# Part of a gather by GpSimd moved to single-row transfers issued by SyncE and ScalarE, in a three-layer graph kernel

## The reference

```python
def _sage_conv(x, src, dst, Wl, bl, Wr):
    agg = jax.ops.segment_max(x[src], dst, num_segments=x.shape[0])
    agg = jnp.where(jnp.isfinite(agg), agg, 0.0)
    return agg @ Wl + bl + x @ Wr
h = jnp.maximum(_layernorm(x, axis=-1), 0.0)
h = leaky_relu(_sage_conv(h, src, dst, Wl1, bl1, Wr1), 0.01)   # 128 -> 256 features
h = leaky_relu(_sage_conv(h, src, dst, Wl2, bl2, Wr2), 0.01)   # 256 -> 256
h = leaky_relu(_sage_conv(h, src, dst, Wl3, bl3, Wr3), 0.01)   # 256 -> 128
out = x + h
```

## Time and profile before

| | |
|---|---|
| median of the three runs | 6152.48 us |
| the profiled execution's own time | 6149.21 us |
| its span, first to last instruction | 6147.2 us |
| POOL busy | 4599.8 us, 75% |
| VectorE busy | 2902.2 us, 47% |
| ScalarE busy | 227.5 us, 4% |
| TensorE busy | 685.4 us, 11% |
| indirect gathers from the feature table | 4692, mean 946 ns |
| DMA moved | 1088.81 MB, 177 GB/s over the span |

### The profile page before, as it was taken

The page is one execution under the profiler, slowest core; times in us unless marked ns, Lnnn a source line. Parts: engine busy times, 40 slices in busy tenths (PEclk is TensorE's granted clock), DMA queues, the critical chain, the costliest instruction groups (busy, mean ns, idle before and its releaser), DMA issues.

```text
span 6147.2 us, 24451 instructions
## 1 busy us (share of the span) xinstructions
PE 685.4 (11%) x2214; PEld 394.3 (6%) x2214; DVE 2902.2 (47%) x3636; ACT 227.5 (4%) x663; POOL 4599.8 (75%) x4874
## 2 busy tenths in 40 slices
PE   0111111111100770000000000056000000000003
PEld 0000000000000430000000000044000000000002
DVE  4333333333333555555555555565555555555556
ACT  1000000000000110000000000011000000000001
POOL 6777777777777777777777777767777777777776
PEclk7555555555555655555555555565555555555556
DMA  4333333333333576666666666667666666666665
GB/s 139 106 109 106 107 107 106 107 107 105 109 104 106 183 234 209 210 210 211 208 211 211 209 210 211 210 213 244 211 211 208 209 211 209 211 208 211 210 208 177
DMA packets 434294, 1088.81 MB, mean 177 GB/s; under 512 B 100294, under 2 KB 152779, under 8 KB 434267
## 3 DMA queue, kind: packets, MB, share of 16 engines
q0 software_dynamic: 206976, 530.17, 30.6%
q1 hardware_dynamic: 204506, 539.02, 23.5%
q10 hardware_dynamic: 22784, 19.34, 1.0%
HBM read 555.06 MB, written 533.07 MB: 177 GB/s over the span
## 4 chain that ended last, share of the span: by engine, by line
POOL 49%; issue 16%; DMA 1%; POOLq 1%; DVE 0%; PE 0%
POOL ring L396 47%; POOL ring L423 2%; POOLq L393 0%; DMA ring<-features,stage 0%; POOLq L390 0%; DMA patch<-running_max_log,patch_row 0%; DMA ring<-running_max_log,end_row 0%; DMA running_max_log<-patch 0%; POOL patch L413 0%; PE banks L987 0%; POOLq L403 0%; POOLq L392 0%; DVE z_sum L841 0%; DMA features<-h_out 0%; DVE ring L731 0%
## 5 line engine op out<-in xcount | busy, mean ns | idle before, releaser
L396 POOL DMA_INDIRECT ring<-features,stage x4692 | 4436.4, 946 | 1456.0 <-issue 1411.4
L731 DVE TENSOR_TENSOR ring<-banks,ring 128x1024 f32<-128x1024 f32 (+1 forms) x1173 | 1226.6, 1046 | 3047.3 <-DMA ring<-features,stage 3030.1
L703 DVE TENSOR_TENSOR banks<-ring,banks 128x1024 f32<-128x1024 f32 (+1 forms) x1173 | 1231.9, 1050 | 37.5
L956 PE MATMUL banks<-ident,ring 128*128 128x128 f32 x20 | 5.0, 427 | 3762.1 <-DVEq L743 3762.1
L930 PE MATMUL banks<-dst_low,own 128*128 128x394 bf16 x200 | 96.0, 480 | 1466.6 <-DVE own L679 1466.6
L956 PEld LDWEIGHTS banks<-ident,ring 128*128 128x128 f32 x20 | 3.9, 222 | 3763.5 <-DVEq L743 3537.2
L914 PE MATMUL banks<-wr,h_turned 128*128 128x256 f32 (+1 forms) x490 | 201.9, 554 | 96.0 <-ACT h_turned L1048 96.0
L1092 ACT ACTIVATE agg<-zeros 128x512 f32<-128x512 f32 x75 | 47.3, 630 | 3944.1 <-PE banks L987 3944.0
L423 POOL DMA_INDIRECT ring<-running_max_log,end_row x147 | 141.5, 962 | 65.4 <-issue 43.9
L684 DVE COPY stage<-edges 128x8 int32 (+1 forms) x588 | 137.2, 233 | 84.8 <-DVE banks L703 25.8
L916 PE MATMUL banks<-b,ones 1*128 1x256 f32 (+1 forms) x294 | 138.8, 568 | 0.0
(11 more groups left out here) (112 smaller groups left out, 566.5 us busy)
## 6 DMA issues: line engine op xcount, KB each, us to landing
running_max_log<-ring SPq DMA_DIRECT2D x782, 512.0 KB, 3.3
running_max_log<-ring SPq DMA_DIRECT2D x391, 256.0 KB, 2.2
ring<-features,stage POOLq DMA_INDIRECT x4692, 2.8
h_in<-features ACTq DMA_DIRECT2D x98, 128.0 KB, 2.7
features<-h_out SPq DMA_DIRECT2D x48, 256.0 KB, 2.3
h_in<-features ACTq DMA_DIRECT2D x49, 64.0 KB, 1.8
out<-h_out SPq DMA_DIRECT2D x24, 128.0 KB, 2.5
ring<-running_max_log,end_row POOLq DMA_INDIRECT x147, 2.9
```

The lines of the kernel that those rows point to most:

```text
L396: pool.indirect_dma_start(ring[:, c * w:(c + 1) * w], None, tables[l], bass.IndirectOffsetOnAxis(ap=stage[:, b, u:u + 1].bitcast(U32), axi ...
L703: dve.tensor_tensor(sum_ps[:, 0:CHAINS * w].rearrange("p (h f) -> p h f", h=CHAINS), group(g - 1).rearrange("p (h f) -> p h f", h=CHAINS), ...
L731: dve.tensor_tensor(group(g), sum_ps[:, 0:CHAINS * w], group(g), ALU.max).then_inc(turn, 1)
```

## The change

In each of the 27 full steps of a layer 160 rows are no longer gathered by POOL: the 128 rows of column 55 and the last 32 rows of column 54. SyncE fetches the first 72 of them and ScalarE the other 88, each by a DMA of its own of one row, whose place in the table is read from SBUF into a register. POOL gathers 54 full columns and the first 96 rows of column 54. The last step of a layer stays as it was.

The places are prepared once: two DMAs with one word per descriptor bring the row numbers of the 27 steps into `row_list` (27 x 160), and VectorE multiplies them by the row size in bytes into `row_at` for each of the two widths. VectorE waits for the rows of both engines ahead of the maximum at g = 13. SyncE issues its rows in nine parts of 8, one behind each of the step's first nine log stores. ScalarE issues its 88 rows in eight parts of 11, ahead of keep_pair of the same number; so keep_pair is now done once per step in all layers.

```diff
+SYNC_ROWS, SYNC_AT_ONCE = 72, 8
+ACT_AT_ONCE = 11
+ROWS = 160
...
+    ROWS_OF = [(0, SYNC_ROWS), (SYNC_ROWS, ROWS - SYNC_ROWS)]
+    FETCHED = [DMA * count for _, count in ROWS_OF]
+    def by_pool(b, last):
+        return width(b, last) - (b == BLOCKS - 1 and not last)
...
+        def row_places(k, engine, i, at, count, w):
+            first = ROWS_OF[k][0] + at
+            _, places = nc.values_load_multi_w_load_instructions(
+                bass.at_runtime_partition(row_at[w][0:1, first:first + count], i), engines=[engine],
+                min_val=0, max_val=(nodes - 1) * w * 4,
+                skip_runtime_bounds_check_because="src numbers rows of the feature table")
+            return places
+        def table_row(l, w, place):
+            return tables[l].rearrange("n f -> (n f)").bitcast(U8)[bass.ds(place, 4 * w)].rearrange("(a b) -> a b", a=1)
+        def row_slot(k, r, w):
+            before, p = divmod(ROWS_OF[k][0] + r, P)
+            c = RING_COLS - 1 - before
+            p += before * (2 * P - ROWS)
+            return ring[p:p + 1, c * w:(c + 1) * w].bitcast(U8)
...
POOL, gather:
-                        for u in range(width(b, last)):
+                        for u in range(by_pool(b, last)):
                             c = b * BLOCK_COLS + u
+                            rows = 2 * P - ROWS if c == RING_COLS - 2 and not last else P
                             pool.indirect_dma_start(
-                                ring[:, c * w:(c + 1) * w], None, tables[l],
+                                ring[0:rows, c * w:(c + 1) * w], None, tables[l],
...
VectorE, preparation and scan_step:
+            dve.wait_ge(list_loaded, 2 * DMA)
+            for w in widths:
+                dve.tensor_scalar(row_at[w][:, :], row_list[:, :], float(4 * w), None, ALU.mult).then_inc(rows_placed, 1)
...
+                        elif g == GROUPS - 1:
+                            dve.wait_ge(act_rows_landed, FETCHED[1])
+                            dve.sem_inc(act_rows_landed, -FETCHED[1])
+                            dve.wait_ge(sync_rows_landed, FETCHED[0])
+                            dve.sem_inc(sync_rows_landed, -FETCHED[0])
...
ScalarE (for i = 0 the wait on logged is left out in the first layer, and rows_placed is waited for):
+                def fetch_rows(i):
+                    act.wait_ge(group_scanned, i * BLOCKS + (FIRSTS * l + 1))
+                    act.wait_ge(logged[BLOCKS - 1], i * (DMA * STORES_OF[BLOCKS - 1]) + LOGGED[BLOCKS - 1] * l)
+                    for first in range(0, ROWS_OF[1][1], ACT_AT_ONCE):
+                        places = row_places(1, mybir.EngineType.Activation, i, first, ACT_AT_ONCE, w)
+                        for r, place in enumerate(places):
+                            act.dma_start(row_slot(1, first + r, w), table_row(l, w, place)
+                                          ).then_inc(act_rows_landed, DMA)
...
-                with act.Fori(0, PAIRS - 2) as j:
+                fetch_rows(0)
+                keep_pair(0, 2)
+                with act.Fori(1, PAIRS - 2) as j:
+                    fetch_rows(j)
                     keep_pair(j, 2)
+                with act.Fori(PAIRS - 2, PAIRS) as j:
+                    fetch_rows(j)
                 keep_pair(PAIRS - 2, PAIR_TILES[-1])
                 keep_pair(PAIRS - 1, 0)
+                with act.Fori(PAIRS, STEPS - 1) as j:
+                    fetch_rows(j)
...
SyncE (fetch_rows(i, g) is the same with 8 rows of sync_rows_landed, after the logs of groups 0 to 8):
+            with nc.allow_non_contiguous_dma(reason="one word of each row to fetch"):
+                for here, there in list_of(src):
+                    sp.dma_start(here, there).then_inc(list_loaded, DMA)
...
+                            if not last and BLOCK_GROUPS * b * SYNC_AT_ONCE < SYNC_ROWS:
+                                fetch_rows(i, BLOCK_GROUPS * b)
...
+                        if not last and (BLOCK_GROUPS * b + 1) * SYNC_AT_ONCE < SYNC_ROWS:
+                            fetch_rows(i, BLOCK_GROUPS * b + 1)
```

More of the change, by code:

```diff
@@ L12 @@
 U32 = mybir.dt.uint32
+U8 = mybir.dt.uint8
 P = 128
@@ L78, in used_blocks @@
         return [b for b in range(BLOCKS) if width(b, last)]
+    ROWS_OF = [(0, SYNC_ROWS), (SYNC_ROWS, ROWS - SYNC_ROWS)]
+    FETCHED = [DMA * count for _, count in ROWS_OF]
+    assert LAST <= RING_COLS - CHAINS and all(f * (STEPS - 1) < 1 << 16 for f in FETCHED)
+    assert SYNC_ROWS % SYNC_AT_ONCE == 0 and (ROWS - SYNC_ROWS) % ACT_AT_ONCE == 0
+    assert SYNC_ROWS // SYNC_AT_ONCE <= GROUPS - 3
+    def by_pool(b, last):
+        return width(b, last) - (b == BLOCKS - 1 and not last)
     OPENING = [CHAINS if b == LATE_BLOCK else width(b, True) for b in range(BLOCKS)]
-    LANDED = [DMA * ((STEPS - 1) * BLOCK_COLS + OPENING[b]) for b in range(BLOCKS)]
+    LANDED = [DMA * ((STEPS - 1) * by_pool(b, False) + OPENING[b]) for b in range(BLOCKS)]
     STORES_OF = [width(b, False) // CHAINS for b in range(BLOCKS)]
@@ L130, in gnn_program @@
         stage = sb("stage", [P, BLOCKS, BLOCK_COLS], I32)
+        row_list = sb("row_list", [STEPS - 1, ROWS], I32)
+        row_at = {w: sb(f"row_at_{w}", [STEPS - 1, ROWS], I32) for w in widths}
         end_row = sb("end_row", [P, TILES], I32)
@@ L260, in gnn_program @@
         LAYERS = len(shapes)
-        LOADS = 6
+        LOADS = 8
         CONSTS = 16 + 2 * CHAINS
@@ L289, in run_neighbours, with list_of @@
             return pairs
+        def list_of(edges_src):
+            pairs = []
+            for first, count, run in ((0, P, (CHAINS - 1) * P), (P, ROWS - P, (CHAINS - 1) * P - (ROWS - P))):
+                chain = run * RUN + GROUPS - 1
+                pairs.append((row_list[:, first:first + count],
+                              bass.AP(edges_src.tensor, chain, [[GROUPS, STEPS - 1], [RUN, count]])))
+            return pairs
+        def row_places(k, engine, i, at, count, w):
[12 more added lines that the diff above has]
+            return ring[p:p + 1, c * w:(c + 1) * w].bitcast(U8)
         block = ctx.enter_context(nc.Block())
@@ L367, in _ @@
                         pool.dma_start(dest, there).then_inc(sort_done, DMA)
+                pool.wait_ge(list_loaded, 2 * DMA)
+                with nc.allow_non_contiguous_dma(reason="one word of each row to fetch"):
+                    for here, there in list_of(sorted_src):
+                        pool.dma_start(here, there).then_inc(sort_done, DMA)
                 pool.wait_ge(sort_done, DMA * (3 + LOADS))
@@ L723, in scan_step @@
                                 keep_lead(1)
-                            dve.wait_ge(landed[b], i * (DMA * BLOCK_COLS) + (LANDED[b] * l + DMA * OPENING[b] if last else
-                                                                               LANDED[b] * l + DMA * BLOCK_COLS))
+                            each = DMA * by_pool(b, False)
+                            dve.wait_ge(landed[b], i * each + (LANDED[b] * l + DMA * OPENING[b] if last else
+                                                               LANDED[b] * l + each))
                         elif last and b == LATE_BLOCK:
@@ L1127, in _, with fetch_rows @@
             for l, (w, n) in enumerate(shapes):
+                def fetch_rows(i, g):
+                    first = g * SYNC_AT_ONCE
+                    if g == 0:
+                        if isinstance(i, int):
+                            sp.wait_ge(rows_placed, len(widths))
+                            if l == 0:
+                                sp.wait_ge(h0_stored, DMA * HEAD_STEPS)
+                            else:
+                                for b in range(STORES):
+                                    sp.wait_ge(h_stored[b], PER_OUT * l)
+                                sp.wait_ge(logged[BLOCKS - 1], LOGGED[BLOCKS - 1] * l)
+                        else:
+                            sp.wait_ge(logged[BLOCKS - 1], i * (DMA * STORES_OF[BLOCKS - 1]) + LOGGED[BLOCKS - 1] * l)
+                    places = row_places(0, mybir.EngineType.SP, i, first, SYNC_AT_ONCE, w)
+                    for r, place in enumerate(places):
+                        sp.dma_start(row_slot(0, first + r, w), table_row(l, w, place)
+                                     ).then_inc(sync_rows_landed, DMA)
                 def log_step(i, last):
@@ L1140, in log_step @@
                                      ).then_inc(logged[b], DMA)
-                with sp.Fori(0, STEPS - 1) as i:
+                        if not last and (BLOCK_GROUPS * b + 1) * SYNC_AT_ONCE < SYNC_ROWS:
+                            fetch_rows(i, BLOCK_GROUPS * b + 1)
+                log_step(0, False)
+                with sp.Fori(1, STEPS - 1) as i:
                     log_step(i, False)
```

9 lines of the change are left out of this document (8 added, 1 removed).

## The result

The changed kernel takes 6050.23 us (median of four runs, 6049.34 to 6051.73) against 6152.78 us before (now four runs, 6151.45 to 6154.44): a ratio of 0.9833, 95% interval 0.9816 to 0.985. That is 102.5 us less, where 117 us were forecast and 6035 us as the time.

What follows compares the result with a forecast made beforehand. POOL's 1.25 us per gather was taken as the bound: 101 us for 81 gathers and 16 us for shorter ones, 117 us off 6149.2 gives 6032, 6035 us as median; range 6020 to 6270 us.

Steps and rivals of the forecast that it cites:

- What bounds the kernel: POOL's gathers, one per 1.25 us, set the 70.0 us step; 81 fewer save 101.2 us.
- The 96-row gather: Column 54's shortened gather on POOL: 0.20 us less each, 16 us in all, since busy time mostly goes with rows.
- case C: POOL's 96-row gather costs what a 128-row one does: 6051 us; inside the forecast, which has chance 0.62 with it.
- ScalarE's share W: ScalarE's issue time per step for eight 11-word register loads and 88 one-row DMAs: 53 us.
- limit of 60.2: ScalarE's rows stay free while their issue time is under 68.5 - 8.3 = 60.2 us; forecast margin 7 us.
- break-even: ScalarE's issue time of 61.7 us per step, at which the change equals the present 70.0 us step.
- rival A: ScalarE's row fetch sets the step through its eight 11-word loads, making the kernel slower, such as 6557 us; chance 0.28.
- The Trainium skill's 0.2 us per register: Page's price for register loads; on ScalarE it gives 63 us of issue, 3 us past the limit, about 6260 us.
- ScalarE's pair work: Work between ScalarE's row fetches: 6.9 us a pair in layer one, shorter in layers two and three.
- the 8.3 us: Rest of ScalarE's row-fetch cycle: last row's landing 2.4 us, then maximum, add, copy and log landing, some 6 us.
- the slip of 4 us over nine groups: SyncE's parts with a log take 5.4 us against POOL's 5.0 per group; logs slip about 4 us, hidden.
- DMA engines, head: Extra rows add 14 us of engine time per step, off POOL's path; list DMAs before VectorE's first scan cost nothing.

Runs made afterwards that it cites:

- e6: Changed kernel with the single rows left out and gathers of 96, 64, 32, 16, 8, 112 and 128 rows in blocks 0 to 6: 5835.5 us, ratio 0.9484.
- e5b: Changed kernel with 256 single rows per step, 128 by each engine, in 16-word loads, POOL gathering 54 columns; undisturbed chip: 6477 us, before 6153, ratio 1.0527.
- e1b: Changed kernel with 128 single rows per step (72 SyncE, 56 ScalarE, loads of 8 words) and a full gather for the other column: 6052.15 us, ratio 0.9826.

## Why the prediction was right, and where it was not

**What bounds the kernel.** Right. POOL's pitch stayed at 1.25 us, the step fell to 68.8 us, and 81 gathers at 1.25 are 101 us.

**The 96-row gather: this term was mis-sized.** I took 0.20 us per gather, 16 us; it is 0.03 us, 2.4 us. That is, to 2 us, case C, which the text had inside the forecast's range: 6051 there, 6050 measured. The reasoning that failed: the duration doesn't follow the bytes, so it follows the rows. It follows neither. From 128 to 16 rows it falls by a tenth (e6). The sign that I named for it, a 96-row form under 946 ns, was too weak: 915 ns is under 946 and confirms 0.03 us, not 0.20.

**ScalarE's share W.** Forecast 53 us, measured 57.6, with a limit of 60.2. That the move worked is in part luck, for two errors nearly cancelled: loads of 11 words at about 3.0 us in layers two and three (8 x 1.1 us more) and rows at 0.32 rather than 0.43 us (88 x 0.11 = 10 us less). The rest, some 5 us, are rows that came slower than 0.32: the first behind a load took 0.57 us and the last ahead of one nearly 0.5, and others were late now and then. With the loads as they are and rows at my 0.43 us, W is 8 x 3.0 + 38 = 62 us, past break-even. The loads alone passed the 2.8 us that I had named as the sign of rival A, and A did not happen. It was closer than I said: 2.6 us, not 7. Its mechanism, a step set by the cycle of the rows, is shown in e5b.

**The Trainium skill's 0.2 us per register** (page "Runtime: NRT & Kernel Launch", section "Instruction fetch mechanics"), given for loads from HBM. The changed kernel's 11 words from SBUF, at 0.25 us each, look like it. On ScalarE 16 words in 1.27 us and 8 in 0.78 don't.

**ScalarE's pair work** takes 8.5 us in layer two (3001.04 to 3009.52), longer than the 6.9 us of layer one, not shorter. It filled the 8.3 us that I had left for it, and the next load came 4.5 us after, at 3014.0.

**SyncE.** Forecast 49 us, measured 44, and the slip of 4 us over nine groups did not come: a part with its log takes 4.3 us (2949.67 to 2953.93), less than the 4.9 of a group. The log of a block's second group goes out some 3 us late, since a part of rows stands ahead of it (maximum done at 2946.83, log at 2949.67), and the next block's is in time again (2955.00, 2955.26). No one waited for the logs. In e5b the parts are longer than a group, and there SyncE decided.

**DMA engines, head.** VectorE's first add is at 44.97 us, against 45.32 before: the list of 4320 words cost nothing that shows. POOL's 100.2 us are 3.5 less than 101.3 + 2.4; these 0.8 ns per gather I did not pursue.

## What to carry to other kernels

When one engine's instruction count is the bound and its instructions have a fixed price, only whole instructions are worth moving; shaving rows off one is hardly worth it (here 0.1 of 1.25 us for 112 rows of 128). Work moved to another queue is free as long as its whole cycle (issue, landing, what must be done before it may start again, and the turn of a long loop) fits into the step, and that cycle, not the busy time, is what to add up. The cycle has to be added up for each engine that takes a share, with that engine's own prices: here one engine's 16-word loads took 1.3 us and the other's 2.1. A version that doubles what is moved must also be checked for what stands behind it in the queue: here the stores.

## What the hardware showed that I had not expected

- An indirect gather is busy for 0.85 us with 16 rows and 0.946 with 128, whether a row has 512 or 1024 bytes, plus 0.30 between two. With 8 rows it takes 0.86, more than with 16 (e6).
- A register load from SBUF doesn't go by its words: on ScalarE 8 words 0.78 us (e1b), 16 words 1.27 (e5b), 11 words 2.75 (the changed kernel), but 1.46 for one of its eight loads. The engine matters too: on SyncE 8 words 1.23 us and 16 words 2.03. So does the layer: SyncE's 8 words take 1.10 us in layer one and 1.40 in the others. What sets the price is not separated.
- A one-row DMA takes 0.23 us to issue, 0.32 us from row to row.
- A loop of 330 instructions on SyncE stood still at its turn for 4.0 and 6.0 us in two layers and 0.2 in the third, one of 220 for 0.2 (medians).
- On two chips single instructions of SyncE, and of ScalarE where it issued rows, took 0.7 or 1.4 us instead of 0.03 us; in the kernels without single rows 0.7 us was the median of SyncE's. The kernel before took 7001 and 7004 us there, and the kernels with single rows were slower than it. The cause stays open; the gain of this change holds for the undisturbed chips.
